# A Runge-Kutta loop on one Trainium2 core: p's terms summed by TensorE, and folded constants

## The reference

```python
xt = jnp.transpose(x, (0, 2, 1))
q, k, v = xt @ Wq[1], xt @ Wk[1], xt @ Wv[1]
scores = jnp.einsum('bqd,bkd->bqk', q, k) * sqrt_dk_inv
scores = scores * hmask + (1.0 - hmask) * -1e+30
attn = jax.nn.softmax(scores, axis=2) * vmask
out = jnp.tile(attn @ v, (1, 1, num_header)) @ Wo
x = x + jnp.transpose(out, (0, 2, 1))
```

```python
def _derivative(q, p, drive, coupling, bias):
    i_couple = jnp.tanh(q) @ coupling.T
    dq = q - q ** 3 / 3.0 - p + drive + i_couple + bias
    dp = EPSILON * (q + ALPHA - BETA * p)
    return (dq, dp)
# four derivatives a step (at 0, DT/2, DT/2, DT), then
q_next = q + DT / 6.0 * (dq1 + 2 * dq2 + 2 * dq3 + dq4)
p_next = p + DT / 6.0 * (dp1 + 2 * dp2 + 2 * dp3 + dp4)
# both clipped to +-20; DT = 0.01, EPSILON = 0.08, ALPHA = 0.7, BETA = 0.8
```

## Time and profile before

| | |
|---|---|
| runs | 6049.42 us median of 3 (6048.22 to 6050.3) |
| profiled execution | 6057.33 us, span 6055.5 us |
| TensorE's granted clock, mean | 0.995 |
| busy: VectorE | 5678.5 us, 94%, 32584 instructions |
| busy: TensorE matmul / weight load | 4516.8 us, 75% / 3815.0 us, 63% |
| busy: ScalarE | 2596.6 us, 43% |

### The profile page before, as it was taken

How to read it: one execution, slowest core, us unless ns; L and a number is a source line. 1 busy time by engine, 2 the same in 40 slices (tenths; PEclk the granted TensorE clock), 3 DMA queues, 4 the chain that set the end, 5 groups by cost and what they waited for, 6 DMA issues and landing times.

```text
span 6055.5 us, 592967 instructions
## 1 busy us (share of the span) xinstructions
PE 4516.8 (75%) x263627; PEld 3815.0 (63%) x263627; DVE 5678.5 (94%) x32584; ACT 2596.6 (43%) x12040; POOL 5.6 (0%) x16
## 2 busy tenths in 40 slices
PE   7887777777777777777777777777777777777777
PEld 3446666666666666666666666666666666666666
DVE  5569999999999999999999999999999999999999
ACT  3334444444444444444444444444444444444444
POOL 0000000000000000000000000000000000000000
PEclk8999999999999999999999999999999999999999
DMA  5100000000000000000000000000000000000000
GB/s 206 44 15 0 0 7 0 7 0 7 0 0 7 0 7 0 7 0 0 7 0 7 0 7 0 0 7 0 7 0 7 0 0 7 0 7 0 7 0 7
DMA packets 11597, 57.06 MB, mean 9 GB/s; under 512 B 2616, under 2 KB 2616, under 8 KB 8512
## 3 DMA queue, kind: packets, MB, share of 16 engines
q1 hardware_dynamic: 11056, 55.84, 2.3%
q10 hardware_dynamic: 528, 1.05, 0.0%
HBM read 40.11 MB, written 16.78 MB: 9 GB/s over the span
## 4 chain that ended last, share of the span: by engine, by line
DVE 81%; issue 8%; ACT 5%; PE 5%; DVEq 1%; DMA 0%; SPq 0%; ACTq 0%
DVE xb L646 44%; DVE turned_sums L796 14%; DVE tanh_parts L646 8%; ACT xb L422 5%; DVE xb L819 5%; DVE xb L855 2%; DVE xb L923 2%; PE ps L493 2%; DVE drive L934 1%; DVE xb L908 1%; DVE xb L884 1%; PE ps L511 1%; DVE xb L914 1%; PE ps L548 1%; PE ps L537 1%
## 5 line engine op out<-in xcount | busy, mean ns | idle before, releaser
L604 PE MATMUL ps<-coup,tanh_parts 128*16 128x96 f16 (+1 forms) x262272 | 4165.0, 219 | 1463.9 <-ACT tanh_parts L428 740.9
L604 PEld LDWEIGHTS ps<-coup,tanh_parts 128*16 128x16 f16 x262272 | 3652.9, 89 | 1976.6 <-ACT tanh_parts L428 924.5
L422 ACT ACTIVATE xb<-xb 128x24 f32<-128x24 f32 (+1 forms) x4098 | 940.4, 230 | 3091.9 <-DVE xb L646 3081.7
L646 DVE SCALAR_TENSOR_TENSOR xb<-xb 128x64 f32<-128x64 f32 x11267 | 2153.5, 214 | 70.0
L646 DVE SCALAR_TENSOR_TENSOR xb<-turned_sums,step_scale,xb 128x64 f32<-128x64 f32 (+2 forms) x6145 | 1561.2, 261 | 41.7 <-issue 0.4
L796 DVE STREAM_TRANSPOSE turned_sums<-ps 128x96 f32<-128x96 f32 (+1 forms) x4096 | 1281.5, 313 | 70.4 <-issue 69.1
L646 DVE SCALAR_TENSOR_TENSOR tanh_parts<-xb,tanh_parts 128x24 f16<-128x24 f32 (+1 forms) x4098 | 717.1, 175 | 15.6
L466 ACT ACTIVATE xb<-xb 128x64 f32<-128x64 f32 x2048 | 499.3, 244 | 0.0
L428 ACT ACTIVATE tanh_parts<-xb 128x24 f16<-128x24 f32 (+1 forms) x2050 | 471.1, 230 | 64.5
L819 DVE SCALAR_TENSOR_TENSOR xb<-xb 128x64 f32<-128x64 f32 x2049 | 450.8, 220 | 0.1
L440 ACT ACTIVATE tanh_parts<-xb 128x24 f16<-128x24 f32 (+1 forms) x2048 | 357.3, 221 | 32.2
(11 more groups left out here) (69 smaller groups left out, 914.7 us busy)
## 6 DMA issues: line engine op xcount, KB each, us to landing
xb<-in_x SPq DMA_DIRECT2D x8, 2048.0 KB, 7.9
drive<-in_x_pt SPq DMA_DIRECT2D x8, 2048.0 KB, 24.5
out_pt<-drive SPq DMA_DIRECT2D x16, 1024.0 KB, 4.5
drive<-in_coupling_t SPq DMA_DIRECT2D x8, 512.0 KB, 11.5
mask_v<-in_cond SPq DMA_DIRECT2D x8, 132.0 KB
probs<-in_wo ACTq DMA_DIRECT2D x1, 1024.0 KB, 5.6
w_qkv<-in_wq SPq DMA_DIRECT2D x1, 64.0 KB, 3.8
w_qkv<-in_wk SPq DMA_DIRECT2D x1, 64.0 KB, 5.2
```

The lines of the kernel that those rows point to most:

```text
L422: nc.scalar.activation(cols(tanh_sb, CHUNKS[j]), cols(q, CHUNKS[j]), ACT.Tanh)\
L604: last = nc.tensor.matmul(product(s, j)[SQ * g:SQ * g + ROWS, :], tanh_parts[:, s % 2, k, :], coup[:, k, part, g, n0:n1, :].rearrange("p c ...
L646: return V.scalar_tensor_tensor(out=out, in0=a, scalar=factor, in1=c, op0=ALU.mult, op1=op1)
```

## The change

p's step becomes g0 x P_SHARES[0] + q_st[0] x P_SHARES[1] + q_st[1] x P_SHARES[2] + q_st[2] x P_SHARES[3], four fp32 matmuls of 64 columns with scaled 128 x 128 unit matrices, summed in PSUM bank 4: two after stage 0's product, one after stage 1's, one after stage 2's. VectorE adds p once the four are in (p_without_last, stage 3, reads PSUM) and the last q (p_next, now behind the second q_of of stage 3). The p sums and rise_of(2) go. Stage 3's step of q is folded so that with_first_part(3) makes the first part from z_rest directly: z_of_last's term in q_st[3] goes into the cubic's constant (OFFSET, CURVE), and q_share's factor changes to Q_KEPT. In the tails of stages 0 and 3 the cubic moves ahead. p_next, clip_p, with_first_part(0) and base_of(0) get a wait or a semaphore of their own. TensorE's loop body holds four stages.

```diff
...
 import concourse.bass as bass
 from concourse import mybir
 from contextlib import ExitStack
+import struct
 F32 = mybir.dt.float32
 F16 = mybir.dt.float16
...
+def single(x):
+    return struct.unpack("f", struct.pack("f", x))[0]
+CURVE = single(-STEP[3] / 3)
+OFFSET = single((STEP[3] + THIRD) / CURVE)
+Q_STEP = [single(THIRD * Q_SUM[1]), single(Q_SUM[2] / Q_SUM[1])]
+Q_KEPT = 1 - THIRD - Q_STEP[0] * Q_STEP[1] - (CURVE * OFFSET - STEP[3] - THIRD)
+P_SHARES = [P_SUM[0], -1 - P_SUM[1] - P_SUM[2], P_SUM[1], P_SUM[2]]
 CHUNKS = [(0, 3), (3, 8)]
 NCH = len(CHUNKS)
...
 SQ = 32
 STRIPS = P // SQ
 ROWS = PARTS * B
-PE_STAGES = 2
+PE_STAGES = STAGES
 UNROLLED = 2
 TANH_SCALE = 4096.0
 COUP_EXP = 14
...
         y = state()
         y_less = state()
         q_share = state()
-        rise = [state() for k in (1, 2)]
+        rise = state()
         q_sum = [state() for k in range(3)]
-        p_sum = [state() for k in range(4)]
+        p_half = state()
+        p_shares = []
+        for k in range(len(P_SHARES)):
+            first = next(states)
+            next(states)
+            p_shares.append(xb[:, :, :].rearrange("p c n -> p (c n)")[:, first:first + P])
         z_rest = state()
         ps = ctx.enter_context(nc.psum_tensor("ps", [P, NBANK, BANK], F32))
...
         z_ready = sem("z_ready")
         z_rest_ready = sem("z_rest_ready")
         p_ready = sem("p_ready")
+        p_shares_ready = sem("p_shares_ready")
+        p_summed = sem("p_summed")
+        p_raw_ready = sem("p_raw_ready")
+        zero_ready = sem("zero_ready")
         q_share_ready = sem("q_share_ready")
         clipped = sem("clipped")
...
         def cols(t, blocks):
             return t[:, B * blocks[0]:B * blocks[1]]
+        p_sum = ps[:, 2 * NCH, 0:COLS]
         def by_block(t, blocks):
             return cols(t, blocks).rearrange("p (c b) -> p c b", b=B)
...
                         first_part_from_forecast(1 - parity, 2.0 if following == 1 else 1.5, act.snap(made >> 1), made)
                     if s == 0:
-                        nc.scalar.activation(q_share[:, :], q_st[0][:, :], ACT.Copy, scale=1 - THIRD)\
+                        nc.scalar.activation(q_share[:, :], q_st[0][:, :], ACT.Copy, scale=Q_KEPT)\
                           .then_inc(q_share_ready, STAGES)
                     now = made
...
                                 tile_position=(0, SQ * g), skip_group_check=True)
                 return last
+            def share_of_p(k, state_of):
+                return nc.tensor.matmul(p_sum, p_shares[k], state_of[:, :], start=(k == 0),
+                                        stop=(k == len(P_SHARES) - 1), skip_group_check=True)
+            pe.wait_ge(p_shares_ready, 1)
             pe.wait_ge(start_ready, NCH + 1)
             for kj, j in ORDER:
...
                         if place == len(ORDER) // 2:
                             after = pe.snap(now + 1)
+                    if s == 0:
+                        pe.wait_ge(base_ready, now)
+                        share_of_p(0, g0)
+                        share_of_p(1, q_st[0])
+                    if s == 1:
+                        share_of_p(2, q_st[1])
+                    if s == 2:
+                        share_of_p(3, q_st[2]).then_inc(p_summed, STAGES)
                     now = after
...
             attend(B - 1, False)
+            for k, share in enumerate(P_SHARES):
+                last = V.tensor_scalar(p_shares[k], ident[:, :], share, None, ALU.mult)
+            last.then_inc(p_shares_ready, 1)
             V.memset(ps[:, 0:2 * NCH, :].rearrange("p a n -> p (a n)"), 0.0)
             V.memset(tanh_parts[:, 1, :, B * REST:B * (REST + 1)], 0.0).then_inc(start_ready, 1)
...
             def cubic_of(stage, made):
                 dve.wait_ge(square_ready, made)
-                V.scalar_tensor_tensor(out=cubic[:, :], in0=square[:, :], scalar=-3.0,
+                V.scalar_tensor_tensor(out=cubic[:, :], in0=square[:, :], scalar=-3.0 if stage < 3 else OFFSET,
                                        in1=q_st[stage][:, :], op0=ALU.add, op1=ALU.mult)\
                  .then_inc(cubic_ready, 1)
-            def base_of(stage, made):
+            def base_of(stage, made, linear=None):
                 dve.wait_ge(cubic_ready, made)
-                axpy(base[:, :], cubic[:, :], -STEP[stage] / 3, z_first_part[:, :]).then_inc(base_ready, 1)
+                if linear is not None:
+                    dve.wait_ge(zero_ready, linear)
+                axpy(base[:, :], cubic[:, :], -STEP[stage] / 3 if stage < 3 else CURVE, z_first_part[:, :]).then_inc(base_ready, 1)
             def with_first_part(stage, out, z_of_stage):
...
             def z_of_third():
-                axpy(z3[:, :], rise[0][:, :], -DT * RISE * G1[1], y_less[:, :])
-            def rise_of(stage):
-                V.tensor_tensor(rise[stage - 1][:, :], q_st[stage][:, :], q_st[0][:, :], ALU.subtract)
+                axpy(z3[:, :], rise[:, :], -DT * RISE * G1[1], y_less[:, :])
+            def rise_of_first():
+                V.tensor_tensor(rise[:, :], q_st[1][:, :], q_st[0][:, :], ALU.subtract)
             def q_sum_g0():
...
             def q_sum_r1():
-                axpy(q_sum[1][:, :], q_sum[0][:, :], DT / 2 / Q_SUM[1], rise[0][:, :])
+                axpy(q_sum[1][:, :], q_sum[0][:, :], DT / 2 / Q_SUM[1], rise[:, :])
             def q_sum_r2():
-                axpy(q_sum[2][:, :], rise[1][:, :], Q_SUM[2] / Q_SUM[1], q_sum[1][:, :])
+                axpy(q_sum[2][:, :], q_st[2][:, :], Q_STEP[1], q_sum[1][:, :])
             def z_without_last(now):
                 dve.wait_ge(q_share_ready, now)
-                axpy(z_rest[:, :], q_sum[2][:, :], THIRD * Q_SUM[1], q_share[:, :])
-            def z_of_last(now):
-                dve.wait_ge(z_rest_ready, now)
-                axpy(z_first_part[:, :], q_st[3][:, :], THIRD, z_rest[:, :])
+                axpy(z_rest[:, :], q_sum[2][:, :], Q_STEP[0], q_share[:, :]).then_inc(z_rest_ready, STAGES)
             def forecast_third(made):
...
             def g0_of():
                 axpy(g0[:, :], p_st[:, :], -BETA, q_st[0][:, :])
-            def p_sum_g0():
-                axpy(p_sum[0][:, :], g0[:, :], P_SUM[0], q_st[0][:, :], ALU.subtract)
-            def p_sum_r(k):
-                axpy(p_sum[k][:, :], rise[k - 1][:, :], P_SUM[k], p_sum[k - 1][:, :])
-            def p_sum_q3():
-                V.tensor_tensor(p_sum[3][:, :], p_sum[2][:, :], q_st[3][:, :], ALU.add)
+            def p_without_last(now):
+                dve.wait_ge(p_summed, now)
+                axpy(p_half[:, :], p_sum, DT / 6 * EPS, p_st[:, :])
             def p_next():
-                axpy(p_raw[:, :], p_sum[3][:, :], DT / 6 * EPS, p_st[:, :])
-            def clip_p():
+                axpy(p_raw[:, :], q_st[3][:, :], DT / 6 * EPS, p_half[:, :]).then_inc(p_raw_ready, STAGES)
+            def clip_p(now):
+                dve.wait_ge(p_raw_ready, now)
                 V.tensor_scalar(p_st[:, :], p_raw[:, :], -CLAMP - SHIFT, CLAMP - SHIFT, ALU.max, ALU.min)\
                  .then_inc(p_ready, STAGES)
...
             dve.wait_ge(start_turned, 1)
             with_first_part(0, z_first_part, z).then_inc(setup, 1)
             dve.wait_ge(setup, 10)
+            g0_of()
             base_of(0, 1)
-            g0_of()
             def stage(s, now):
...
                 turn_product(s, 0, now)
                 if s == 0:
                     y_of()
-                if s == 1:
-                    z_of_third()
                 if s == 2:
-                    p_sum_r(2)
+                    q_sum_r2()
                 if s == 3:
-                    p_next()
+                    p_without_last(now)
                 q_of(s, 0, now)
                 if s == 0:
                     z_of_second()
                 if s == 1:
-                    p_sum_g0()
-                if s == 2:
-                    z_without_last(now)
+                    z_of_third()
                 if s == 3:
                     look_ahead((now + STAGES) * (COLS // STAGES))
                 turn_product(s, 1, now)
                 rest_of(parity, 0, made)
                 q_of(s, 1, now)
                 if s == 0:
+                    q_sum_g0()
                     y_less_g0()
-                    q_sum_g0()
                 if s == 1:
                     q_sum_r1()
-                    p_sum_r(1)
                     drive_step_of((now + 2) * (COLS // STAGES))
                 if s == 2:
-                    with_first_part(3, z_rest, z_rest).then_inc(z_rest_ready, STAGES)
+                    z_without_last(now)
                     trace((now - 3) * (COLS // STAGES))
                 if s == 3:
-                    clip_p()
+                    p_next()
                     clip_q(made)
-                    drive_less_p(now)
+                    clip_p(now)
                 rest_of(parity, 1, made)
                 if s == 0:
                     forecast_third(made)
```

(17 more changed lines are left out.)

## The result

6106.25 us median (6103.76 to 6108.35, 4 runs) against 6049.86 us for the kernel before (6048.22 to 6052.74): ratio 1.0093, 95% interval 1.0075 to 1.011. The forecast was 6113 us (+1.1%). The profiled execution's span is 6102.0 us against 6055.5.

The account below looks back on a forecast made before the run. VectorE's order bounds the kernel, with a TensorE floor of 2.63 us a stage. Per two steps 2 x 0.32 - 0.27 - 0.12 = +0.25, x 256 = +64 us: 6121 profiled, 6113 median (+1.1%); range 6055 to 6160.

Parts of the forecast that it names:

- stage 1: Window of stage 1, 17 to 13 VectorE instructions: falls from 2.76 to the floor of 2.63 us, -0.13.
- stage 2: Window of stage 2, 15 to 13 VectorE instructions: already at the floor of 2.63 us, so 0.
- stage 3: Window of stage 3, 16 to 17 VectorE instructions: grows from 2.75 to 3.07 us, +0.32 a step.
- stage 0, first: First stage 0 of a loop iteration: stays 2.71 us, 0 taken, with 0.17 of VectorE idle left unnamed.
- stage 0, with the branch: Second stage 0, followed by the loop's branch: base starts earlier, 2.96 falls to 2.84 us, -0.12 an iteration.
- two steps: One loop iteration of eight stage windows: from 21.95 to 22.2 us, +0.25.
- The floor: Every stage: TensorE alone sets at least 2.63 us, which taking instructions off VectorE can't pass.
- The price in stage 3: Tail of stage 3: p_next ahead of clip_p and new waits delay the transpose by 0.32 us a step.
- the cubic's new place: Stage 3's tail: cubic ahead of with_first_part saves nothing, since with_first_part waits for z longer than the cubic lasts.
- p_without_last: Stage 3, reads PSUM: cost 0, hidden behind the transpose; up to 0.06 us a step if not covered.
- The shares: TensorE's passes for p, 0.13 us each: covered by its pauses of 0.73 and more, 0; uncovered 530 us.
- The larger loop on TensorE: TensorE's four-stage loop body: not fetched again each time; rival of refetching once a step, 7540 us, chance 0.04.

Follow-up runs that it names:

- Experiment 3: Changed kernel with p_without_last moved to stage 2, p_next and clip_p to stage 3's first half, z waiting for clip_q alone: 5892.83 us, ratio 0.9735 to the kernel before.
- experiment 4: Changed kernel plus unused VectorE subtractions at the ends of stages 1 and 2: one in each 6134.02 us, two in each 6211.4 us.
- second run of experiment 9: Experiment 3's kernel with p's sum as three VectorE terms instead of TensorE shares, the first term placed behind drive_step: 5900.06 us, ratio 0.9745.
- first run of experiment 9: Experiment 3's kernel with p's sum as three VectorE terms instead of TensorE shares, the first term in stage 1's first half: 5960.58 us, ratio 0.9848.
- experiment 2: Changed kernel with p_next behind stage 3's first q_of, that stage's tail in its old order, look_ahead in stage 2: 5937.53 us, ratio 0.9809.
- experiment 1: Changed kernel with the cubic put back between with_first_part(0) and base_of(0), without semaphore zero_ready: 6125.72 us, ratio 1.0119.
- experiment 6: Changed kernel with each of the four TensorE shares done a second time into another PSUM bank: 6106.12 us, ratio 1.0094.
- experiment 5: Kernel before with only TensorE's loop changed, four stages a turn in place of two: 6051.89 us, ratio 1.0005.
- experiment 7: Kernel before with 80 empty VectorE instructions ahead of the loop, shifting its code: 6019.29 us, ratio 0.9949.

## Why the prediction was right

Term by term, each per occurrence:

| term | forecast | measured |
|---|---|---|
| stage 1 | 2.63 (-0.13) | 2.63, 2.63 |
| stage 2 | 2.63 (0) | 2.64, 2.64 |
| stage 3 | 3.07 (+0.32) | 3.07, 3.08 |
| stage 0, first | 2.71 (0) | 2.63 (-0.08) |
| stage 0, with the branch | 2.84 (-0.12) | 2.82 (-0.14) |
| two steps | 22.20 | 22.14 |

*The floor* held. Experiment 3 brings all stages to it, the single spare instructions of experiment 4 vanish into it, and the second run of experiment 9 adds three instructions a step for a thousandth. But it isn't TensorE's alone, as the prediction has it. In stage 1 of the changed kernel 1.26 us pass from the opening transpose to TensorE's next start and 1.37 from there to the next opening transpose (3001.42, 3002.68, 3004.05), and the 1.26 hold VectorE's first half with ScalarE's tanh. An instruction too many there lengthens the stage, 2.77 in the first run of experiment 9. Whether a shorter first half would bring the floor down no run tried.

*The price in stage 3* held link by link: the tail grew by the 0.32 worked out, and experiment 2 takes it away by bringing p_next forward. That the cubic's new place saves nothing was right; experiment 1 measures it at 0.01.

*p_without_last* was hidden, as forecast, and its PSUM input costs next to nothing: 0.19 us, where the instruction in the same place before, with both inputs in SBUF, took 0.18. In experiment 3, between trace and rest_of, it takes 0.22 like its neighbours from SBUF. The time of such an instruction goes with its place, and the 0.06 allowed for PSUM wasn't needed.

```profile
3006.89 0.19 DVE L688 SCALAR_TENSOR_TENSOR xb<-ps,xb 128x64 f32<-128x64 f32 x1
```

*The shares* cost nothing, even twice (experiment 6). Their passes come 0.11 apart rather than the 0.13 used.

*The larger loop on TensorE* cost nothing (experiment 5). The Trainium skill, Advanced Engine Details and Errata, ISA Cache, was on the right side there.

*The one term off* is the first stage 0, given as 0 with 0.17 of idle that I couldn't name. In the kernel before it holds the stall of experiment 7; in the changed kernel no stage shows the stall, -0.08 x 256 = 20 us, and where it went no run tells. The prediction had allowed 23 us either way for this idle time. The 20 are more than the whole of the 15 us between the forecast's two-step sum, +64, and the 49 of the windows; the other windows, off by 0.01 to 0.02 each, give 5 back. The medians differ by 56 and the profiled spans by 46.5, since the profiled execution before lies 8 us above its median and the one after 2.5 below its own. So the mechanism was right term by term, and that 6113 comes as near as 7 us to 6106 is in part luck.

The rule of the Trainium skill, VectorE: DVE Perf Modes, Rules for kernel authors, to minimize the number of operations and not the semaphores, doesn't give even the sign here: with five operations fewer the kernel is 0.9% slower, since one of those that stayed moved into a chain. Between kernels with the same 58 the places of the operations on p and behind it, and of the waits, are worth 3.5% (6106 to 5893).

## What to carry to other kernels

In a loop that goes round several engines, find for each stage which engine is just in time, and spend nothing on taking work off the others there: first see whether the instructions removed stood in its shadow. An operation that moves into a chain of dependent small ones costs its whole duration and a wait (here 0.22 + 0.11 us), so bring forward what doesn't depend on the latest value; that was worth 3% with no work saved. Where it goes matters as much: an instruction that no longer fits before the second transpose was paid in full (0.14), the same one moved behind the second q_of cost 0.02. A program that does the same in the same order can differ by 0.5% by where its code lies, so a small gain from a reordering wants its windows read, not its time alone.

## What the runs showed that was not expected

- A stall of 0.09 to 0.10 us once a loop on VectorE that goes with where the code lies, its cause open: 80 empty instructions ahead of the loop took 30 us off the kernel before (ratio 0.9949). It surfaced in stage 0, in stage 3, or nowhere, in kernels that differ by a few instructions.
- A scalar_tensor_tensor of 64 columns took 0.18 to 0.22 us by its place in the order, and an input in PSUM changed that by 0.01 at most.
- A late start of a stage can be made up in its first half: two spare instructions in each of two stages cost 0.12 in one and 0.05 us in the other.
